# Four conditional layers, 32 batches in 16 pairs: a pair's second matrix is split in one piece, its last two loads and the table reads move on SyncE

## The reference, cut to what matters

```python
# x: (32, 64, 1024); four integers for each of the 32 batches
def L0(x, w, bias, A, B, scale, id):      # 8 adapters, rank 16
    return einsum('bsi,oi->bso', x, w) + bias \
         + scale[id][:, None, None] * einsum('bsr,bor->bso', einsum('bsi,bri->bsr', x, A[id]), B[id])
def L1(x, id, w, bias, A, B):             # 32 adapters, rank 16
    return einsum('bsd,od->bso', x, w) + bias + einsum('bsr,bor->bso', einsum('bsd,brd->bsr', x, A[id]), B[id])
def L2(x, w, id): return einsum('bsi,boi->bso', x, w[id])        # 8 matrices of 1024 x 1024
def L3(x, w, id): return einsum('bct,bcd->bdt', x, w[id])        # 16 matrices of 64 x 64
x = x + L0(x, ..., itok_B_1_7)
x = x + L1(x, itok_B_6_15, ...)
x = x + L2(x, L2_weight, itok_B_3_7)      # ids 3 to 7: five matrices are used
x = x + L3(x, L3_weights, itok_B_0_15)
```

## Time and profile before

| | |
|---|---|
| median of 3 runs | 591.07 us (591.01 to 591.71) |
| the profiled execution | 594.11 us |
| span in its trace, first to last instruction | 592.3 us |
| mean granted TensorE clock | 0.991 |
| PE busy | 575.4 us (97%) |
| DVE / ACT / POOL busy | 326.2 / 281.0 / 52.4 us |
| DMA | 60.93 MB, mean 103 GB/s |

### The profile page before, as it was taken

One profiled execution on the slowest core, in us unless ns is written; L12 is line 12 of the kernel. 1 busy time (PEld: TensorE's weight loads), 2 busy tenths in 40 slices (PEclk: granted clock), 3 DMA queues, 4 the chain that ended last, 5 costly groups with the idle time before them and its releaser, 6 DMA issues.

```text
span 592.3 us, 10814 instructions
## 1 busy us (share of the span) xinstructions
PE 575.4 (97%) x2710; PEld 480.1 (81%) x2711; DVE 326.2 (55%) x583; ACT 281.0 (47%) x370; POOL 52.4 (9%) x87
## 2 busy tenths in 40 slices
PE   8999999999999999999999999999999878999997
PEld 7888888888877888888888888888888766788885
DVE  6984212023786568655646865555686655746320
ACT  5632211016564648636255863635586238254312
POOL 3340000200100300000110000011010201000000
PEclk9999999999999999999999999999999988899999
DMA  8755826010216233372313336231343630211103
GB/s 311 258 178 60 99 88 220 10 45 18 90 52 239 73 89 103 88 240 74 80 46 91 114 90 230 67 91 36 91 124 101 220 107 28 66 51 38 36 2 72
DMA packets 66015, 60.93 MB, mean 103 GB/s; under 512 B 42050, under 2 KB 50242, under 8 KB 65988
## 3 DMA queue, kind: packets, MB, share of 16 engines
q1 hardware_dynamic: 65988, 60.63, 34.9%
HBM read 49.33 MB, written 11.27 MB: 102 GB/s over the span
## 4 chain that ended last, share of the span: by engine, by line
PE 85%; SPq 5%; issue 3%; DVE 3%; DMA 1%; ACT 1%; POOL 0%; ACTq 0%; DVEq 0%; POOLq 0%
PE y_ps L1310 25%; PE y_ps L1268 25%; PE y_ps L1218 11%; PE t_ps L1218 6%; PE t_ps L1299 4%; PE y_ps L1199 2%; SPq L241 2%; PE low_ps L1258 2%; PE y_ps L1195 1%; PE t_ps L1199 1%; PE low_ps L1199 1%; PE y_ps L1283 1%; PE y_ps L1284 1%; PE y_ps L1324 1%; PE t_ps L1209 1%
## 5 line engine op out<-in xcount | busy, mean ns | idle before, releaser
L1268 PE MATMUL y_ps<-wm,ops 128*128 128x512 f32 x768 | 181.4, 394 | 0.0
L1268 PEld LDWEIGHTS y_ps<-wm,ops 128*128 128x128 f32 x768 | 143.0, 189 | 29.4 <-DVE arena L997 0.2
L1310 PE MATMUL y_ps<-ring,ops 128*128 128x512 f32 x696 | 165.3, 390 | 0.0
L1310 PEld LDWEIGHTS y_ps<-ring,ops 128*128 128x128 f32 x696 | 128.9, 188 | 25.5
L575 ACT CAST ops<-arena 128x512 fp32r<-128x512 f32 x32 | 19.7, 620 | 96.0 <-PE y_ps L1268 96.0
L1218 PE MATMUL y_ps<-ring,wm 128*128 128x512 f32 x240 | 55.3, 390 | 0.0
L1218 PEld LDWEIGHTS y_ps<-ring,wm 128*128 128x128 f32 x240 | 44.9, 188 | 9.3
L990 DVE TENSOR_TENSOR ring<-arena,ring 128x1024 fp32r<-128x1024 f32 x40 | 47.5, 1221 | 4.4 <-ACT ring L606 3.7
L606 ACT CAST ring<-arena 128x1024 fp32r<-128x1024 f32 x40 | 40.5, 1050 | 6.8 <-POOL arena L477 4.2
L997 DVE TENSOR_TENSOR arena<-y_ps,bias 128x1024 f32<-128x1024 f32 x16 | 19.6, 1225 | 41.0 <-PE y_ps L1284 40.9
L1004 DVE TENSOR_TENSOR arena<-arena,ops 128x512 f32<-128x512 f32 x32 | 23.0, 718 | 31.0 <-ACT arena L629 30.4
(11 more groups left out here) (153 smaller groups left out, 638.9 us busy)
## 6 DMA issues: line engine op xcount, KB each, us to landing
arena<-wt SPq DMA_DIRECT2D x48, 512.0 KB, 4.4
arena<-xt SPq DMA_DIRECT2D x32, 256.0 KB, 2.7
out<-arena SPq DMA_DIRECT2D x30, 256.0 KB, 3.1
arena<-w SPq DMA_DIRECT2D x8, 576.0 KB, 5.4
a_stage<-a_tab SPq DMA_DIRECT2D x64, 64.0 KB, 1.9
arena<-b_tab SPq DMA_DIRECT2D x64, 64.0 KB, 2.0
arena<-a_cols SPq DMA_DIRECT2D x8, 256.0 KB, 4.2
a_tab<-bias SPq DMA_DIRECT2D x4, 256.0 KB, 8.4
```

The source lines that it names most:

```text
L1268: op = nc.tensor.matmul(y_ps[:, cols], xs[:, k, part_x, :], wm[:, k, part_w, cols], start=k == 0 and part_x == part_w, stop=False)
L1310: op = nc.tensor.matmul(y[:, cols], xs2[:, k, part_x, :], ring[:, k, part_w, cols], start=k == 0 and part_x == part_w, stop=k == KT - 1 an ...
```

## The change

On ACT and DVE `behind_layer2` splits all eight tiles of a second matrix, and only then evicts the first transposes of the next pair; before it split four, evicted, and split the other four. On PE the second transposes of such a pair come behind its last layer 2 matmuls, not ahead of the last four. On SP the loads of tiles 6 and 7 of a second matrix get a function of their own (`rest_of_second`) and stand with `after_next` ahead of `x_and_a`; `b_rows` moves to the end of the step ahead (`b_rows(j + 2)` at the end of step j is what `b_rows(j + 1)` was at the start of step j + 1) and takes the LoRA numbers that `x_and_a` has read. DVE's `take_out(j - 2)` moves from the head of a step behind `sum_low(j, 1)`. In a pair with one matrix ACT signals `first_copied` and `first_taken` a little earlier.

```diff
@@ SP @@
+            def rest_of_second(j):
+                second = second_of(sp, j)
+                with sp.If(second != 0):
+                    other_chunks(second)
+
             def behind_layer2(j):
-
                 second, following = second_of(sp, j), next_of(sp, j)
                 with sp.If(second != 0):
-                    other_chunks(second)
                     first_chunks(second + 1)
                 with sp.If(following != 0):
                     other_chunks(following)
@@
             def step(j):
-                b_rows(j + 1)
                 store(j - 2)
                 layer3_of(j + 1)
-                x_and_a(j + 2)
                 after_next(j - 2)
+                rest_of_second(j - 1)
+                which = x_and_a(j + 2)
                 behind_layer2(j - 1)
+                b_rows(j + 2, which)
@@ ACT @@
                 with act.If(second != 0):
-                    convert_second(second, j, FIRST_HALF)
+                    convert_second(second, j, range(KT))
                 with act.Else():
+                    act.sem_inc(first_copied, 1)
+                    act.sem_inc(first_taken, 1)
                     if not last:
                         b_hi_parts(j + 2)
                 xs2_hi(j + 1, 0, its_second)
                 with act.If(second != 0):
-                    convert_second(second, j, SECOND_HALF)
                     act.wait_ge(stored, 32 * j + 16)
                     copy_first(j)
@@ DVE @@
                 with dve.If(second != 0):
-                    convert(second, FIRST_HALF)
+                    convert(second, range(KT))
@@
                 xs2_lo(j + 1, 0, its_second)
                 with dve.If(second != 0):
-                    convert(second, SECOND_HALF)
                     add_first(j)
@@
-                take_out(j - 2)
                 sum_low(j, 0)
                 split_low(j, 0)
                 couple(j)
                 sum_low(j, 1)
+                take_out(j - 2)
                 xs2_lo(j - 1, 1, second)
@@ PE, batch_half and layer2 @@
-                        if between and k == KT - 1:
-                            between(1)
@@
-                        batch_half(y2_ps, 1, 0, between=between)
+                        batch_half(y2_ps, 1, 0)
+                        between(1)
```

More of the change, by code:

```diff
@@ L375, in x_and_a, with b_rows @@
                 load_a(which)
-            def b_rows(j):
-                which = loras(j)
+                return which
+            def b_rows(j, which):
                 sp.wait_ge(b_lo, 2 * j)
@@ L401, in step @@
             def step(j):
-                b_rows(j + 1)
                 store(j - 2)
                 layer3_of(j + 1)
-                x_and_a(j + 2)
                 after_next(j - 2)
+                rest_of_second(j - 1)
+                which = x_and_a(j + 2)
                 behind_layer2(j - 1)
-            x_and_a(1)
+                b_rows(j + 2, which)
+            which = x_and_a(1)
             other_chunks(0)
-            b_rows(1)
+            b_rows(1, which)
             layer3_of(1)
-            x_and_a(2)
+            which = x_and_a(2)
             first_chunks(1)
-            b_rows(2)
+            b_rows(2, which)
             layer3_of(2)
-            x_and_a(3)
+            rest_of_second(0)
+            which = x_and_a(3)
             behind_layer2(0)
+            b_rows(3, which)
             with sp.Fori(2, PAIRS - 2) as j:
                 step(j)
-            b_rows(PAIRS - 1)
             store(PAIRS - 4)
@@ L427, in _ @@
             after_next(PAIRS - 4)
+            rest_of_second(PAIRS - 3)
             behind_layer2(PAIRS - 3)
@@ L431, in _ @@
             after_next(PAIRS - 3)
+            rest_of_second(PAIRS - 2)
             behind_layer2(PAIRS - 2)
@@ L435, in _ @@
             after_next(PAIRS - 2)
-            second = second_of(sp, PAIRS - 1)
-            with sp.If(second != 0):
-                other_chunks(second)
+            rest_of_second(PAIRS - 1)
             batches = of_pair(T_BATCH, BATCHES - 2, BATCHES - 1)
@@ L697, in behind_layer2 @@
                         b_hi_parts(j + 2)
-                with act.Else():
-                    act.sem_inc(first_copied, 1)
-                    act.sem_inc(first_taken, 1)
                 with act.If(following != 0):
@@ L1329, in layer2, with batch_half @@
                 rank, second = first_rank(pe, i), second_of(pe, i)
-                def batch_half(to, h, batch, tiles=False, between=None):
+                def batch_half(to, h, batch, tiles=False):
                     for k in (FIRST_HALF, SECOND_HALF)[h]:
```

## The result

The changed kernel takes 582.25 us (median of 4 runs, 581.91 to 582.34) where the kernel before took 591.16 us beside it (591.01 to 591.71): ratio 0.9846, 95% interval 0.9833 to 0.9859, 8.9 us faster. The forecast was 579.1 us with a range of 578.2 to 582.4; the time lies at the upper edge of the range, and the gain is three quarters of the 12.0 us that the sum gave. Yet nearly every place of the trace is where the prediction put it.

The account below looks back on a forecast made before the run. PE, busy 97%, was taken as bound, with gains only in its gaps and low clock. Profiled 594.11 less 12.0 us gives 582.1, less 3.04 to the median 579.1 us; range 578.2 to 582.4, widened for a returning wait.

Parts of the forecast that it names:

- the sum: First two-matrix matmul to next layer 2: 29.4 us, was 41.38, so 12.0 us less: 5.6 waits, 3.6 clock, 2.8 smaller gaps.
- the two causes: PE's 3.81 us wait for the second matrix: tiles 4 and 5 split after an eviction, tiles 6 and 7 loaded late.
- The margin of 1.8 us: Tile 7 of the second matrix: DVE's split ends by 484.6 us at worst, PE wants it at 486.4.
- the median is 3.04 us below its profile: Last step of the forecast: profiled execution 582.1 us less 3.04 us gives a median of 579.1 us.
- 3.6 us the low clock: Slow matmuls behind the waits for `ring` and `g_split`, 1.9 and 1.7 us too much, counted as gain.
- rival 2: SP's loads come no earlier; only the `g_split` wait and its slow stretch go: 587.6 us, chance 0.05.
- rival 1: A wait of about 1 us comes back at `g_split` or tile 7, with a clock drop: 581.8 us, chance 0.14.
- What was costed at nothing: SP's other moves, ACT's signals in pairs with one matrix and PE's moved transposes: no time gained or lost.
- at most 0.4 us: In the other steps only one DVE read changes its place, costing no more than 0.4 us.
- The rule that was weighed: Two-input DVE operations lock out POOL's folds for a whole instruction; by the rows at most 1.1 us more a fold.

Follow-up runs that it names:

- experiment 2: Kernel before with only SP's load order as changed, all other engines as before: 588.96 us, ratio 0.9954.
- experiment 3: Kernel before with only ACT's, DVE's and PE's order as changed, SP as before: 591.38 us, ratio 0.9994.
- experiment 5: Changed kernel with the loads of tiles 6 and 7 back behind the x and A loads: 585.07 us, ratio 0.9902.
- experiment 4: Changed kernel with DVE's `take_out` back at the head of the step: 584.42 us.
- experiment 11: Kernel before, unchanged, traced again: one execution of 591.75 us.
- experiment 1: Kernel before, unchanged, run again: 591.19 us over 12 runs, ratio 1.0; its traced run took 593.66 us.
- experiment 12: Kernel before, unchanged, traced once more: one execution of 592.07 us.
- experiment 6: Changed kernel with the four reads of the LoRA numbers back in `b_rows`: 582.23 us, ratio 0.9845.
- 9: Changed kernel with PE's second transposes back between tile 6 and tile 7: 582.57 us.
- first profile: Kernel before, unchanged, the traced execution on which the prediction was built: 594.11 us.
- experiment 10: Kernel before with ACT's, DVE's and PE's order as changed, SP as before, plus 24 unused matmuls ahead of PE's wait for tile 6: 590.61 us, ratio 0.9988.

## Why the prediction was right in its places and off in its size

**What bounds the kernel, and the two causes.** Right. SP's issue came at 475.39 (475.5 foreseen), the folds at 478.73 and 481.31 (479.3 and 480.9), the last split of DVE ended at 485.15 (483.6 to 484.6, so 0.5 us later than the worse of the two), the eviction at 486.5 (486.2), the low products began at 488.16 (488.0), `g_split` was ready at 492.8 (493.6), the next layer 2 began at 501.08 (500.9). The fold of tile 7 was put too early by the prediction's own numbers: it took 5.4 us from SP's coming to tile 6 for tile 7 as well, though its line before had tile 7's load wait for a second split of DVE, 1.1 us later than tile 6's. The margin of 1.8 us took that up. Experiments 2 and 3 show that neither part does it alone, 5 that the loads' place counts for 2.8 us, 4 that `take_out`'s place counts for 2.2 us.

**The sum.** The step that failed is "the median is 3.04 us below its profile, 591.07, and I forecast 579.1 us". I took those 3.04 us for a constant between a profile and a timed run. They were a slow passage through just the stretch that the change mends. Against experiment 11 it has 1.5 us of a fold that came late and met a split and 1.6 us of low clock behind `g_split`, and 0.75 us less ahead of step 2, which together are the 2.4 us between the two executions. A change that removes the waits removes them too, and a median that never had them can't lose them. The forecast for the profiled execution, 582.1 us, was right to 0.2 us, because nothing of the kind happens in the changed kernel: its nine runs lie between 581.91 and 582.68 us. The term "3.6 us the low clock" was thus mis-sized for the median: of it the 1.6 us behind `g_split` are in none of the three other traces of before (experiments 1, 11 and 12); for the median the sum of 12.0 us is 8.9. The same mistake put experiments 2 and 3 and rival 2 some 3 us too low. The range held, since it had been widened upward for rival 1, a wait that did not come; for the real reason it was luck.

**What was costed at nothing.** The saved reads (experiment 6) and the place of the transposes (9): right. DVE's moved read cost more than the "at most 0.4 us": 0.84 us of issue ahead of the eviction at 461.76, the read and its branch. It is covered. In a step that splits a new matrix the read is gone from the head, where DVE's idle time fell from 1.58 us to 0.67: the transposes there still begin 18.35 us after the low products (431.28 to 449.63), as in the earlier trace rows (431.17 to 449.52).

**The fold beside a split.** The rule that was weighed, that of the Trainium skill (SBUF — State Buffer, section "SBUF: two separate sides"), is borne out by durations: 0.45 or 0.46 us for a fold that meets no split (experiments 5, 11 and 12), 1.41 and 1.50 us in the changed kernel, where DVE's seven splits run back to back over both. Folds that met a split ended 0.30 to 0.32 us behind the end of it, in the first profile (491.96 and 491.66), in experiment 1 (492.63 and 492.32) and in the changed kernel (480.14 and 479.82, 482.81 and 482.49). The split next in line paid too, 1.48 us where the others take 1.22 or 1.23:

```profile
479.74 1.48 DVE L994 TENSOR_TENSOR ring<-arena,ring 128x1024 fp32r<-128x1024 f32 x1
```

Neither fold was held off by more than a split of about 1.2 us, so the sum was right to go by the rows, and tile 7's split ended 1.1 us ahead of its matmuls (487.21 less four matmuls of 0.23 is 486.3), inside the 0.6 to 1.8 us foreseen. The prediction saw the clash in the earlier trace rows, but not that it was part of what made that execution a slow one.

**The rivals.** None came. The waits for `ring`, `g_split` and the transposes are gone; SP was in time; the steps with one matrix are still 25.75 us (431.28 to 457.03). That rival 1's wait at `g_split` would have come with `take_out` at its old place is shown by experiment 4.

**What stays open.** Why the runs spread when PE is kept busy through the wait (experiment 10), and single late runs (587.42, 595.3 us), for which there is no trace. The 1.3 us ahead of step 2 can be a part of it. That a late landing of tile 7 carries into the time is read from four traces of the kernel before; no run delayed a landing and changed nothing else.

## What to carry to other kernels

Before a gain is subtracted from a median, ask where the profiled execution differs from the median: if it was slower, the surplus can lie in the waits that it shows, as it did here, and then goes with them. Count on the stretch as an ordinary run has it, or forecast for the profiled execution and say so. And where two causes stand one behind the other, cost the parts alone as well: here they gave 2.5 and 0 us alone, and 8.9 together; with the waits the spread of 3 to 5 us from run to run went too (nine runs of the changed kernel within 0.8 us).

## What the runs showed of the hardware that was not expected

- The same gap in PE's work does not always cost the clock. Behind a wait of 1.76 us for `g_split` the granted clock was 0.64 from 505 to 509 us, behind one of 1.46 us in another execution of the same kernel 1.00, and 1.00 behind 1.80 us in experiment 4. Behind 3.81 us it was at 1.2 GHz in each of the four traces of before (8 matmuls in 3.78 us), but the place where it rose again differed: the low products some 8 to 11 us behind that wait took 1.10 or 1.11 us in three executions of the kernel before and 1.91 us in another. Low clock there costs little while a later wait takes it up: 1.55 us later at the low products was 0.31 us at the next layer 2 (experiments 12 and 11).
- A late transfer can cost more than its lateness: a fold that began 0.4 us later in the stretch met a DVE split, went from 0.46 to 1.51 us, and `g_split` came 1.48 us later. Where it met none, 0.31 us stayed 0.31 us.
